# Layer-0 local scores over 64 rows: two head-group halves in two PSUM banks, units in pairs

## The reference, cut to what matters

```python
Qb = Q.reshape(Bx, H, nb, W, D)                       # H 16, W 32, D 8, nb 32
Kw = jnp.concatenate([Kp[:, :, :-1], Kp[:, :, 1:]], axis=3)   # the window before and the own one: 64 keys
Vw = jnp.concatenate([Vp[:, :, :-1], Vp[:, :, 1:]], axis=3)
sc = jnp.einsum('bhnid,bhnjd->bhnij', Qb, Kw) / np.sqrt(D)
sc = jnp.where(mask[None, None], sc, -jnp.inf)
p = jax.nn.softmax(sc, axis=-1)
out = jnp.einsum('bhnij,bhnjd->bhnid', p, Vw)
...
out = gl * local + gr * rem                           # rem: attention to 64 latents, 8 heads
return out @ w_out
```

## Time and profile before

| | us |
|---|---|
| median of 3 runs | 406.0 (402.62 to 406.39) |
| profiled execution, its own time | 403.82 |
| its span in the trace | 401.4 |
| PE busy in the span | 352.3 (88%) |
| DVE busy | 256.6 (64%) |
| POOL busy | 205.2 (51%) |
| ACT busy | 177.5 (44%) |

### The profile page before, as it was taken

How to read it: one execution, slowest core, us unless ns; L and a number is a source line. 1 busy time by engine, 2 the same in 40 slices (tenths; PEclk the granted TensorE clock), 3 DMA queues, 4 the chain that set the end, 5 groups by cost and what they waited for, 6 DMA issues and landing times.

```text
span 401.4 us, 8798 instructions
## 1 busy us (share of the span) xinstructions
PE 352.3 (88%) x2593; PEld 319.0 (79%) x2609; DVE 256.6 (64%) x786; ACT 177.5 (44%) x486; POOL 205.2 (51%) x267
## 2 busy tenths in 40 slices
PE   0899898999999989997897899999999999999910
PEld 0598787988899978876786555999999999999900
DVE  5775998776311669789678897875774444444416
ACT  1715443444556534434454782334334444444304
POOL 8214444898545738692301207444546886642320
PEclk9989999999999999998999989999999999999975
DMA  7781000010362300001010153987888999898137
GB/s 240 268 296 27 0 2 3 21 33 26 106 211 93 123 5 2 0 2 53 19 71 19 53 159 105 308 248 225 264 245 260 287 293 280 288 282 261 69 109 225
DMA packets 33197, 56.01 MB, mean 140 GB/s; under 512 B 4192, under 2 KB 11680, under 8 KB 33152
## 3 DMA queue, kind: packets, MB, share of 16 engines
q1 hardware_dynamic: 28704, 46.14, 36.7%
q0 software_dynamic: 3872, 8.27, 6.3%
q10 hardware_dynamic: 576, 1.05, 0.8%
HBM read 46.59 MB, written 8.85 MB: 138 GB/s over the span
## 4 chain that ended last, share of the span: by engine, by line
PE 62%; DVE 14%; issue 8%; POOL 6%; ACT 4%; DMA 4%; SPq 1%; ACTq 0%; DVEq 0%; POOLq 0%
PE bank L1322 16%; PE bank L1306 8%; PE bank L1035 4%; PE bank L1331 4%; PE bank L997 4%; PE bank L1091 4%; PE bank L1077 3%; DVE rmax L1551 3%; PE bank L1019 2%; PE bank L875 2%; POOL shared L474 2%; POOL shared L468 2%; PE bank L1007 2%; DMA xn<-y_rows 2%; DMA cb<-in_cb 2%
## 5 line engine op out<-in xcount | busy, mean ns | idle before, releaser
L1322 PE MATMUL bank<-kf,shared 128*128 128x128 f32 x624 | 76.0, 275 | 0.0
L1322 PEld LDWEIGHTS bank<-kf,shared 128*128 128x128 f32 x624 | 73.3, 192 | 0.4
L572 POOL DMA_INDIRECT y_rows<-rows,to x39 | 38.5, 988 | 50.6 <-DVE rows L1822 49.6
L1035 PEld LDWEIGHTS bank<-shared 128*128 128x128 f32 x344 | 44.8, 192 | 9.3 <-issue 6.5
L1815 DVE SCALAR_TENSOR_TENSOR we<-bank,bcol,we 128x128 f32<-128x128 f32 x78 | 23.7, 346 | 41.2 <-ACT we L849 39.8
L1035 PE MATMUL bank<-shared 128*128 128x128 f32 x344 | 46.9, 277 | 2.9 <-DVE remn L1595 2.3
L566 POOL DMA_INDIRECT rows<-xn_rows,from x39 | 38.0, 975 | 18.6 <-issue 11.7
L849 ACT ACTIVATE we<-bank,bcol 128x128 f32<-128x128 f32 x78 | 24.4, 364 | 51.6 <-PE bank L1322 51.6
L1551 DVE TENSOR_REDUCE rmax<-bank 128x8 f32<-128x512 f32 (+2 forms) x48 | 30.2, 630 | 26.6 <-PE bank L997 20.0
L1306 PE MATMUL bank<-xtT,shared 128*128 128x128 f32 x312 | 41.4, 276 | 0.5 <-ACT xtT L842 0.4
L1306 PEld LDWEIGHTS bank<-xtT,shared 128*128 128x128 f32 x312 | 38.0, 192 | 1.2 <-ACT xtT L842 0.6
(11 more groups left out here) (258 smaller groups left out, 695.5 us busy)
## 6 DMA issues: line engine op xcount, KB each, us to landing
shared<-in_w1s SPq DMA_DIRECT2D x39, 512.0 KB, 4.7
shared<-in_w1s SPq DMA_DIRECT2D x39, 256.0 KB, 4.1
we<-in_we SPq DMA_DIRECT2D x8, 514.0 KB, 3.4
xn_rows<-xn SPq DMA_DIRECT2D x12, 256.0 KB, 2.4
x<-in_x SPq DMA_DIRECT2D x4, 256.0 KB, 3.6
y_rows<-kf POOLq DMA_DIRECT2D x4, 256.0 KB, 5.8
w1s<-in_w1s SPq DMA_DIRECT2D x2, 512.0 KB, 8.0
xn<-y_rows SPq DMA_DIRECT2D x4, 256.0 KB, 4.2
```

Of the source, the lines that this page charges most:

```text
L572: pool.indirect_dma_start(out=y1_rows, in_=ysb[:, i % 4, :], in_offset=None, out_offset=bass.IndirectOffsetOnAxis(ap=to1[:, i:i + 1].bitca ...
L1035: mm = pe.matmul(bank[4 + g % 2][:, P * i:P * i + P], probT[:, g % 2, P * i:P * i + P], v_, start=True, stop=True)
L1322: mm = pe.matmul(bank[(1, 3)[(k - 1) % 2]][:, P * f:P * f + P], wglb[:, (k - 1) % 4, a, P * f:P * f + P], zT2[:, (k - 1) % 2, a, :], start ...
```

## The change

The local scores of two units, g and g + 1, are made together. Features 0 to 63 (head groups 0 and 1) go to bank 0, features 64 to 127 (groups 2 and 3) to bank 1, each with matmuls over 64 partitions only. A bank now holds 4 windows of 2 head groups where it held 2 windows of 4; `kd` needs two copies where it needed four. The masks, the place of the value copies (`vd`) and the way in which the weighted results are copied out follow that layout. `shift`, `turn`, `exponent` and `weigh` go bank by bank as before. The pair waits for the shifts of both units before it, and it stands once in the order where two `scores` stood.

```diff
-    f["mine_u"] = p[:, None] // 32 == np.arange(4)[None]
+    f["mine_u"] = p[:, None] // 32 % 2 == np.arange(2)[None]
...
-    b["spread"] = p[:, None] == p[None] % WIN
+    b["spread"] = p[:, None] % 64 == p[None] % WIN
...
             def split_heads(n):
...
-                for u in range(4):
-                    pool.tensor_scalar(kd[:, r, u, :], kT[:], c("mine_u", 4)[:, u:u + 1], None, ALU.mult).then_inc(s_kd, 1)
+                for u in range(2):
+                    pool.tensor_scalar(kd[:, r, u, :], kT[:], c("mine_u", 2)[:, u:u + 1], None, ALU.mult).then_inc(s_kd, 1)
...
             def values(n):
...
-                    act.copy(vd[rows, n % 2, :, 33 * blk:33 * blk + 32], bank[6][rows, :].rearrange("p (g c) -> p g c", c=32)).then_inc(s_vd, 1)
+                    act.copy(vd[rows, n % 2, :, 64 * blk:64 * blk + 32], bank[6][rows, :].rearrange("p (g c) -> p g c", c=32)).then_inc(s_vd, 1)
...
             def weighted(n, u):
...
-                act.copy(oall_flat[n % 2].rearrange("p (r b u c) -> p r u b c", r=NP2, b=2, u=4)[:, u],
-                         bank[4 + g % 2][:].rearrange("p (u x) -> p u x", u=4)[:, :, 0:66].rearrange("p u (b c) -> p u b c", b=2)).then_inc(s_ol, 1)
+                half, pair = divmod(u, 2)
+                act.copy(oall_flat[n % 2].rearrange("p (r b h u c) -> p r h u b c", r=2, b=4, h=2, u=2)[:, half, pair],
+                         bank[4 + g % 2][:].rearrange("p (u b x) -> p u b x", u=2, b=4)[:, :, :, 0:33]).then_inc(s_ol, 1)
...
-            def scores(g):
+            def local_scores(g):
                 n, u = divmod(g, U)
-                to, r = bank[g % 2], n % 2
+                r = n % 2
                 if g >= 2:
-                    pe.wait_ge(s_sub, g - 1)
...
+                    pe.wait_ge(s_sub, g)
...
+                for h in range(2):
+                    rows = slice(64 * h, 64 * h + 64)
+                    pe.matmul(bank[h][:], cbf("spread", P)[rows], cbf(mask, 512)[rows], start=True, stop=False, skip_group_check=True)
+                for blk in range(4):
+                    at = WIN * (2 * u + blk)
+                    for h in range(2):
+                        rows = slice(64 * h, 64 * h + 64)
+                        mm = pe.matmul(bank[h][:].rearrange("p (u b j) -> p u b j", u=2, b=4)[:, :, blk, :],
+                                       qd[rows, r, 2 * u + blk].rearrange("p h i -> p (h i)"), kd[rows, r, :, at:at + 2 * WIN],
+                                       start=False, stop=(blk == 3), skip_group_check=True)
+                        if blk == 3:
+                            mm.then_inc(s_S, 1)
...
+            def remote_scores(g):
+                n, u = divmod(g, U)
+                pe.wait_ge(s_sub, g - 1)
...
-            pe.wait_ge(s_xTs, 3)
-            scores(0)
             pe.wait_ge(s_xTs, 4)
-            scores(1)
+            local_scores(0)
             logits0(0)
             for n in range(NC):
...
                     turn(g)
-                scores(g + 2)
...
                     weigh(g - 1)
+                local_scores(g + 2)
                 turn(g + 1)
-                scores(g + 3)
                 weigh(g)
...
                 turn(g + 2)
-                scores(g + 4)
+                remote_scores(g + 4)
...
                 turn(g + 3)
-                scores(g + 5)
+                remote_scores(g + 5)
...
                 turn(g + 4)
-                if more:
-                    scores(g + 6)
                 weigh(g + 3)
                 if n:
                     project(n - 1)
+                if more:
+                    local_scores(g + 6)
                 turn(g + 5)
-                if more:
-                    scores(g + 7)
...
 (VectorE)
                 if more:
-                    shift(g + 6)
                     sums(n + 1)
                 if n == 0:
                     slot_factors(0, T, J0)
                 if more:
+                    shift(g + 6)
                     shift(g + 7)
```

More of the change, by code:

```diff
@@ L124, in constants @@
     b["local"] = np.where(np.tile(local, (1, 8)), 0, NEG)
-    b["first"] = np.where(np.tile(np.concatenate([local & (j >= WIN), local], 1), (1, 4)), 0, NEG)
+    b["first"] = np.where(np.tile(np.concatenate([local & (j >= WIN), local, local, local], 1), (1, 2)), 0, NEG)
     cf, cb = np.zeros((P, NCF), np.float32), np.zeros((P, NCB), mybir.dt.np(BF16))
@@ L230, in program @@
         rout1, sumR = sb("rout1", [P, P]), sb("sumR", [P, P])
-        shared = sb("shared", [P, 15520])
+        shared = sb("shared", [P, 14368])
         w1s = sb("w1s", [P, E, WS])
@@ L647, in second_keys @@
                 act.wait_ge(s_kT, 2)
-                for u in range(4):
-                    act.activation(kd[:, 1, u, :], kT[:], ACT.Copy, scale=c("mine_u", 4)[:, u:u + 1]).then_inc(s_kd1, 1)
+                for u in range(2):
+                    act.activation(kd[:, 1, u, :], kT[:], ACT.Copy, scale=c("mine_u", 2)[:, u:u + 1]).then_inc(s_kd1, 1)
             def latents(n):
@@ L745, in _ @@
                 if n == 1:
-                    act.wait_ge(s_kd1, 4)
+                    act.wait_ge(s_kd1, 2)
                 if more:
@@ L976, in gates @@
                 mm.then_inc(s_gates, 1)
-            def scores(g):
+            def local_scores(g):
                 n, u = divmod(g, U)
-                to, r = bank[g % 2], n % 2
+                r = n % 2
                 if g >= 2:
-                    pe.wait_ge(s_sub, g - 1)
[L983 to L996, removed]
-                        mm = pe.matmul(to[:].rearrange("p (u b j) -> p u b j", u=4, b=2)[:, :, blk, :],
-                                       qd[:, r, 2 * u + blk].rearrange("p h i -> p (h i)"), kd[:, r, :, at:at + 2 * WIN],
-                                       start=False, stop=(blk == 1), skip_group_check=True)
-                else:
-                    if u == UL:
-                        pe.wait_ge(s_gq, n + 1)
-                        pe.wait_ge(s_gkd, n + 1)
-                    if g == UL:
-                        pe.wait_ge(s_const, 9)
-                    at, nl = n % NCH * CH + P * (u - UL), P // REPS[n % NCH]
-                    mm = pe.matmul(to[:, 0:LH * nl].rearrange("p (h n) -> p h n", h=LH), gqx[:, at:at + P], gkd[:, :, 0:nl], start=True, stop=True)
-                mm.then_inc(s_S, 1)
@@ new lines, in local_scores @@
+                    pe.wait_ge(s_sub, g)
+                if u == 0:
+                    if n == 0:
+                        pe.wait_ge(s_heads0, 6)
+                    else:
+                        pe.wait_ge(s_qd, 4 * n)
+                    if n == 1:
+                        pe.wait_ge(s_kd1, 2)
+                    elif n:
+                        pe.wait_ge(s_kd, 2 * (n - 1))
+                mask = "first" if u == 0 and n % NCH == 0 else "local"
+                for h in range(2):
+                    rows = slice(64 * h, 64 * h + 64)
+                    pe.matmul(bank[h][:], cbf("spread", P)[rows], cbf(mask, 512)[rows], start=True, stop=False, skip_group_check=True)
@@ new lines, in remote_scores @@
+            def remote_scores(g):
+                n, u = divmod(g, U)
+                pe.wait_ge(s_sub, g - 1)
+                if u == UL:
+                    pe.wait_ge(s_gq, n + 1)
+                    pe.wait_ge(s_gkd, n + 1)
+                if g == UL:
+                    pe.wait_ge(s_const, 9)
+                at, nl = n % NCH * CH + P * (u - UL), P // REPS[n % NCH]
+                pe.matmul(bank[g % 2][:, 0:LH * nl].rearrange("p (h n) -> p h n", h=LH), gqx[:, at:at + P], gkd[:, :, 0:nl],
+                          start=True, stop=True).then_inc(s_S, 1)
@@ L1189, in _ @@
                     project(n - 1)
+                if more:
+                    local_scores(g + 6)
                 turn(g + 5)
-                if more:
-                    scores(g + 7)
-                else:
+                if not more:
                     pe.wait_ge(s_xTs, 6)
@@ L1628, in first_heads @@
                 dve.wait_ge(s_kT, 1)
-                for u in range(4):
-                    dve.tensor_scalar(kd[:, 0, u, :], kT[:], c("mine_u", 4)[:, u:u + 1], None, ALU.mult).then_inc(s_heads0, 1)
+                for u in range(2):
+                    dve.tensor_scalar(kd[:, 0, u, :], kT[:], c("mine_u", 2)[:, u:u + 1], None, ALU.mult).then_inc(s_heads0, 1)
             dve.wait_ge(s_xTs, 1)
```

16 lines of the change are left out of this document (8 added, 8 removed).

## The result

The changed kernel took 412.8 us, median of four runs (411.88 to 413.67); the kernel before, run beside it, 405.2 (402.62 to 406.39). The ratio is 1.0213 [1.0165, 1.0261]: slower by about 8 us. The forecast was 408.0, plus 2. In the profiled executions the span grew from 401.4 to 410.1.

What follows compares the result with a forecast made beforehand. TensorE was taken to set a chunk's pace, VectorE close behind. Chunk terms, from +4.5 in chunk 0 to -2.0 in chunk 4, summed to +2.0: 405.8 on the profiled 403.8, plus 2.2 to the median, 408.0 us; range 401 to 420.

Steps and rivals of the forecast that it cites:

- the forecast's own range, 403 to 412: Whole kernel: range in us around the likeliest case, 408.0, which was given a chance of 0.42.
- the empty array: Rival, TensorE at both ends of a pair: each change between half and full rows costs 0.17, 412 us; chance 0.15.
- the one behind the experts: Chunk 4: no wait before weigh(g), its divisions being done in the experts; 2.0 us gained.
- The matmuls: Local scores on TensorE: overlapping halves free 0.96 us per pair, 15.4 in all.
- P: Length of one pair of local score units on TensorE: 1.2 us, bounds 1.1 and 2.2.
- The rival without overlap: Rival, score pairs: halves or their weight loads do not overlap, P 2.0 to 2.2, 419 to 422 us; chance 0.25.
- The wait of weigh(g): TensorE in each chunk: weigh(g) waits 1.73 us for the first remote division, behind shift(g+2) on VectorE.
- Chunk 0: First chunk: VectorE's expert choice and later work stand ahead of the shifts, turn(6) starts near 46.2, 4.5 us lost.
- chunk 6's wait: TensorE's wait for shift(42): 0.65 us lost as next chunk's sums stand ahead; half clock after it expected the same.
- The key copies: POOL makes two instead of four per chunk; TensorE's wait behind the layer-0 experts goes, gaining 1.9 us in that chunk.

Runs made afterwards that it cites:

- Experiment 2: Changed kernel with both remote divisions of the chunk before put ahead of shift(g+2) on VectorE; 403.2 us, ratio 0.9993.
- Experiment 11: Changed kernel with eight useless matmuls in each of three TensorE waits, to keep it at full clock; 408.7 us, ratio 1.016.
- experiment 4: Kernel before, with its 128-row matmuls and four key copies, issued in the pairs' order on TensorE and VectorE; 410.8 us, ratio 1.0176.
- experiment 1: Changed kernel with all eight passes of bank 0 first, then all eight of bank 1; 409.5 us, ratio 1.0165.
- experiment 10: Kernel before with VectorE's divisions and onto_stream moved ahead of shifts and slot factors behind, as far as its banks allow; 401.7 us, ratio 0.9956.
- experiments 6 and 9: 6: changed kernel with VectorE's divisions, expert choice, stream addition and slot factors moved, 393.8 us; 9: same moves on the kernel before issued in pairs' order, 402.9 us.
- experiment 3: Changed kernel with layer 0's expert choice ahead of shift(2) on VectorE, in chunk 0 only; 409.0 us, ratio 1.0167.

## Why the prediction was wrong in size and right in its mechanism

The forecast was no change (plus 2 us); measured was plus 8. That is inside the range of 401 to 420, but only thanks to the rivals: the forecast's own range, 403 to 412, misses it, and the 412 of the empty array was reached by another sum. The mechanism, that the pairs' order hands TensorE's gain to VectorE, held in six chunks of seven; in the one behind the experts it was forecast not to show, and doesn't. By its steps:

- **The matmuls: right.** P was 1.2 and measured 1.21 (in chunk 2 at 71.81 and at 84.66). The rival without overlap is out.
- **The wait of weigh(g): right.** 1.73 was worked out from the chain shift, division, turn. In the trace TensorE's starts are 73.02 and 75.13, 2.11 apart where a turn alone takes 0.44: 1.67. Experiment 2 shows that it carries the slowdown, with the clock that comes with it: 403.2 instead of 412.5.
- **Chunk 0: the right place, too small.** 4.5 was forecast and 6.1 came, 4.6 at full clock. The steps on VectorE fit: the choice ran from 32.53 to past 36.56, forecast 32.8 to 36.8. What was left out is what TensorE did after standing idle. Its waits, and the weighing at half clock behind them:

```profile
37.05 0.22 PE L909 MATMUL bank<-chosen_bf,cb 128*128 128x128 bf16 x1 [1.99 <-DVEq L1430]
...
38.47 1.11 PE L1028 MATMUL bank<-cf,shared 128*128 128x128 f32 x4 [1.14 <-DVE shared L1559]
...
39.80 1.91 PE L1044 MATMUL bank<-shared 128*128 128x128 f32 x8
```

- **The step that failed: the clock was priced only where it fell before.** The prediction said of the half clock "I expect the same there", for chunk 6's wait, and gave the waits that the change adds none. The earlier trace rows held the pattern: 0.58 behind a wait of 2.28. The change makes waits of 1.99 and 1.14 in chunk 0, behind the expert choice, and lengthens the one ahead of turn(12) from 1.5 to 2.3, and the clock fell behind both, to 0.56 and 0.61. Eight passes of 128 columns (L1044) take 1.91 there and 1.06 at full clock. Experiment 11 puts it at 3.8 us of the 8, of which up to 1.7 is what the kernel before pays in chunk 7 as well. The Trainium skill ("TensorE: Matmul & The Clock Gate", section "HAM oscillation — how this bites in real kernels") describes groups of matmuls that each start cold because a wait of 3 to 5 us stands ahead of each. The rows above agree in kind; here waits of 2.0 and 2.3 us were followed by half clock.
- **The ends of a pair: a rival that was true in part.** "The array stands empty at both ends" was given 0.17 per change as a case of its own. At full clock the four passes ahead of a pair take 0.54 to its first mask (84.12 to 84.66), where the same four before a full-row mask take 0.44 (experiment 4, 83.38 to 83.82); the turn behind it takes 0.49 against 0.44. So 0.10 on the way in and 0.05 on the way out, 0.15 a pair, 2.4 us in sixteen, of which the waits hide some. It is the same in sequence (80.52 to 81.06, and 82.82 to 83.32, in experiment 1), so it goes with the change of rows and not with the overlap. The Trainium skill ("TensorEngine Tiling (Array Packing)", section "Key Properties") says that changing the tiling mode drains TensorE; it gives no time, and the 0.15 fits it.
- **The key copies: right that the wait goes, and two copies are not needed for it.** Experiment 4 has all four copies and no wait, experiment 10 four and 3.8 us of wait. The order alone is enough; what the copies alone would give is not shown.
- **No overlap, 419 to 422: mispriced.** P does not stand twice on the round, the time to the first complete bank does. Experiment 1 made the pair longer by 0.55 and nothing slower; experiment 4 came to 410.8 where this arithmetic had its expectation at 424 to 426.
- **Missed: the keys of the next chunk wait for `onto_stream`.** It stands behind both shifts of the pair on VectorE, and these now come right after one another, once the pair is done. In the changed kernel:

```profile
88.37 0.59 PE L950 MATMUL bank<-xnT,wts 128*128 128x256 f32 x2
89.09 0.75 PE L953 MATMUL bank<-xnT,wts 128*128 128x288 f32 x2
```

The keys start 0.72 behind the step before them instead of 0.43, and VectorE's `onto_stream` (88.63 to 89.04) is what they waited for: 0.29 here, and 1.6 in three places by the waits of the weight loads. It is read from the trace; no experiment moved it alone.

With the terms as measured, the forecast's 2.0, the clock's 2.1 to 3.8, up to 1.6 for the keys and up to 2.4 for the ends of the pairs lie between 4 and 10, and the spans are 8.7 apart. Only the clock's was taken apart on the chip; the last two are read from rows, and how much of them stood on the path stays open. Open too is why the half clock comes behind some waits of 2 us and not behind others (last section).

## What to carry to other kernels

When a change fills two buffers at once instead of one after the other, ask first when the earliest consumer can start: issuing them together delays the first bank to the end of the pair and bunches the consumer's work behind it. Then walk the consumer's queue in order and put ahead of that bunch everything that is ready already; here the new matmuls were worth 9 us with VectorE's queue rearranged (experiments 6 and 9) and nothing without (412.5 against the 410.8 of experiment 4), while the pairs' order alone cost 7. Price each new wait of TensorE with the clock that may fall behind it, not by its length alone.

## What the runs showed of the hardware

- Matmuls on rows 0 to 63 and 64 to 127, into two banks, overlap with f32 weights loaded anew for each pass: sixteen passes of 128 columns in 0.98 us (72.04 to 73.02) against 1.54 in sequence (68.44 to 69.98). One half alone is 1.54 / 2 = 0.77, so 0.56 of a possible 0.77 is hidden.
- In sequence the passes on 64 rows are paced at 1.54 / 16 = 0.096, a little under the 0.11 of full-row passes of the same size.
- Some waits of 2.0 to 2.3 us were followed by half clock, once with only 0.3 us of small matmuls between one wait of 1.99 and one of 1.14; the stretches at half clock behind them lasted 3.4 to 6.8 us, with TensorE busy 85 to 100 per cent of them. Others were not: 2.49 ahead of turn(6) in experiment 11, 2.40 in the same place in experiment 3, and 2.20 ahead of turn(42) in experiment 2 left the clock at full. The very same wait of 2.49 ahead of turn(6) in experiment 2 was followed by 3.4 us at 0.52 (48.90 to 52.30). So the length of a wait alone did not decide it in these traces.
